# The combine stage of a soft mixture-of-experts kernel: token groups in a ring of chunks, exponentials in PSUM, row maxima spread by one fp32r product

## The reference

```python
x = x + 0.5 * ffn(layernorm(x))      # f1 in the profile
x = x + attention(layernorm(x))      # at
x = x + 0.5 * ffn(layernorm(x))      # f2

def ffn(x):
    logits   = einsum("bnd,esd->bnes", norm(x), se)
    dispatch = softmax(logits, over tokens)
    combine  = softmax(logits, over all 1024 slots)
    slots    = einsum("bnd,bnes->besd", x, dispatch)
    eout     = experts(slots)                      # [b, 1024, 256]
    return einsum("bns,bso->bno", combine, eout)   # the combine stage
```

## Time and profile before

| | |
|---|---|
| median of 3 runs | 2116.95 us (2116.89 to 2117.19) |
| profiled execution, first to last instruction | 2117.7 us; no other time is given for that execution |
| combine stage of f2, first instruction to last matmul | 1898.7 to 2112.8 us |
| PE busy | 1879.6 us, 89% |
| DVE busy | 1510.7 us, 71% |

### The profile page before, as it was taken

One profiled execution on the slowest core, in us unless ns is written; L12 is line 12 of the kernel. 1 busy time (PEld: TensorE's weight loads), 2 busy tenths in 40 slices (PEclk: granted clock), 3 DMA queues, 4 the chain that ended last, 5 costly groups with the idle time before them and its releaser, 6 DMA issues. The chain is left out here.

```text
span 2117.7 us, 35275 instructions
## 1 busy us (share of the span) xinstructions
PE 1879.6 (89%) x11782; PEld 1661.7 (78%) x11782; DVE 1510.7 (71%) x3055; ACT 1017.6 (48%) x2057; POOL 679.2 (32%) x619
## 2 busy tenths in 40 slices
PE   1799999988699899968999968999999859989999
PEld 1678787877699699968999846878778649978998
DVE  5777777763588899944555467767776348889997
ACT  0044445456455577734343302444354645547775
POOL 1422221100366455512222133212220007745553
PEclk9999999999899899988999979999999989998999
DMA  2353233320355466731212135332332115536774
GB/s 80 145 194 128 92 139 129 120 100 21 125 193 184 154 239 241 258 122 45 75 59 71 43 128 202 134 140 99 119 130 100 70 60 193 176 132 225 262 261 163
DMA packets 96785, 293.78 MB, mean 139 GB/s; under 512 B 7712, under 2 KB 47520, under 8 KB 84384
## 3 DMA queue, kind: packets, MB, share of 16 engines
q1 hardware_dynamic: 96672, 292.39, 38.9%
HBM read 183.31 MB, written 109.05 MB: 138 GB/s over the span
## 5 line engine op out<-in xcount | busy, mean ns | idle before, releaser
L76 POOL TENSOR_TENSOR pool_carrier<-minus_half 128x1 f32<-128x1 f32 x108 | 23.4, 217 | 668.9 <-DVE f2r_mv L352 289.4
L366 DVE TENSOR_SCALAR_CACHE_REDUCE f2r_lt<-f2r_ps_l,slot_shift 128x512 f32<-128x512 f32 x128 | 95.5, 747 | 87.3 <-PE f2r_ps_l L570 69.1
L366 DVE TENSOR_SCALAR_CACHE_REDUCE f1r_lt<-f1r_ps_l,slot_shift 128x512 f32<-128x512 f32 x128 | 95.5, 747 | 86.7 <-PE f1r_ps_l L570 68.6
L1122 PE MATMUL f2c_ps_y<-f2c_eo,f2c_e_hi 128*128 128x258 f32 (+1 forms) x512 | 151.0, 300 | 3.4 <-ACT f2c_e_hi L1078 3.2
L1122 PE MATMUL f1c_ps_y<-f1c_eo,f1c_e_hi 128*128 128x258 f32 (+1 forms) x512 | 151.1, 300 | 2.8 <-ACT f1c_e_hi L1078 2.7
L1123 PE MATMUL f1c_ps_y<-f1c_eo,f1c_e_hi 128*128 128x256 f32 (+1 forms) x512 | 143.8, 286 | 0.0
L1123 PE MATMUL f2c_ps_y<-f2c_eo,f2c_e_hi 128*128 128x256 f32 (+1 forms) x512 | 143.7, 286 | 0.0
L1133 PE MATMUL f1c_ps_y<-f1c_eo,f1c_e_lo 128*128 128x258 f32 (+1 forms) x512 | 135.7, 285 | 0.0
L1133 PE MATMUL f2c_ps_y<-f2c_eo,f2c_e_lo 128*128 128x258 f32 (+1 forms) x512 | 135.7, 285 | 0.0
L518 ACT ACTIVATE f2r_e_hi<-f2r_ps_t 128x512 fp32r<-128x512 f32 x128 | 69.7, 594 | 101.3 <-PE f2r_ps_t L583 101.2
L518 ACT ACTIVATE f1r_e_hi<-f1r_ps_t 128x512 fp32r<-128x512 f32 x128 | 69.7, 594 | 101.3 <-PE f1r_ps_t L583 101.2
(11 more groups left out here) (289 smaller groups left out, 6666.4 us busy)
## 6 DMA issues: line engine op xcount, KB each, us to landing
logits<-f1r_lt SPq DMA_DIRECT2D x16, 2048.0 KB, 7.3
f1c_lt<-logits SPq DMA_DIRECT2D x32, 1024.0 KB, 7.4
logits<-f2r_lt SPq DMA_DIRECT2D x16, 2048.0 KB, 7.3
f2c_lt<-logits SPq DMA_DIRECT2D x32, 1024.0 KB, 7.2
f1r_xin<-in_L_attn_x SPq DMA_DIRECT2D x16, 512.0 KB, 5.2
normalized<-f1r_xin SPq DMA_DIRECT2D x16, 512.0 KB, 2.6
f1r_xback<-normalized SPq DMA_DIRECT2D x16, 512.0 KB, 8.0
f1e_raw_g<-in_L_ffn_Wg SPq DMA_DIRECT2D x16, 512.0 KB, 4.1
```

The costliest lines, as they stand in the source:

```text
L76: pool.tensor_tensor(c["pool_carrier"][:, col:col + 1], c["minus_half"][:, 0:1], c["minus_half"][:, 0:1], ALU.add)
L366: dve.tensor_scalar(lt[:, g, sc, :], ps_l[sc % 2][:, :], c["slot_shift"][:, sc:sc + 1], None, ALU.add, ALU.max, accum_out=gmax[:, sc, g:g ...
L1122: pe.matmul(ps_y[t][:, 0:LO], e_hi[par][:, sc, tile], eo[:, bpar, sc, 0:LO], start=sc == 0, stop=False)
```

## The change

- **PE by chunks.** For chunks 0 to 5 PE takes all four tiles of a chunk in turn (`by_hi`, then `by_lo` of the chunk before). The rest (chunks 6 and 7, and `e_lo` of 5 to 7) it takes tile by tile, so that the tiles end one after the other.
- **One ring.** `e_hi` and `e_lo` have one buffer each. ACT writes chunk sc of the next group when PE has used chunk sc of this one (`chunk_used`; for 5 to 7, `mixed`).
- **One stream on the other engines.** They go from a group into the next without a break, chunk by chunk. On DVE, step sc is: F3 of the group before at sc 0; F1 at sc 7; `e_lo` of chunk sc+1 if it is DVE's; shift of chunk sc+3 (`AHEAD`); F0 after step 6, F2 after step 7. On ACT: exponential of chunk sc+1, `e_hi` of chunk sc, and after chunks 3 and 7 one `slot_out_hi`. On POOL: `e_lo` of chunks 1, 3, 5, 7, with one `slot_out_lo` after chunk 1 and one after chunk 3.
- **PSUM.** The exponentials of DVE's chunks (now 0, 2, 4, 6) are written to two PSUM banks `ps_e`, and read there for `e_hi` and `e_lo`.
- **Row maxima.** At the head of the expert stage they are split in two fp32r parts, transposed by PE and stored to memory as rows. The combine stage loads two rows for each group into a buffer of zeros, and one fp32r product with ones adds and spreads them. The diagonals on POOL go.
- **Transfers.** The logits of group i+2 are asked for in halves, each when POOL is done with that half of group i.
- **Start.** DVE does three shifts before it splits the first batch's expert outputs; PE waits for both.

```diff
+    BY_POOL = (1, 3, 5, 7)
+    TAIL = 5
+    AHEAD = 3
...
+        e_hi, e_lo = al.sb("e_hi", [P, NSC, GN], F32R), al.sb("e_lo", [P, NSC, GN], F32R)
+        ps_e = [al.ps(f"ps_e{i}", [P, BANK]) for i in range(2)]
...
 SP
+                        for h in range(2):
+                            sp.wait_ge(lo_by_pool, len(BY_POOL) * i + (h + 1) * len(BY_POOL) // 2)
+                            load_logits(i + 2, g % 2, h)
+                            if h == 0:
+                                load_max_rows(i + 2, g % 2)
...
 POOL
                     for m, sc in enumerate(BY_POOL):
+                        lo_part(i, g % 2, sc)
                         if exists(b, 0, NG) and m < NSC // NG:
                             slot_out_lo(b + 1, (b + 1) % 2, NSC // NG * g + m)
...
 DVE
+            for sc in range(AHEAD):
+                shift(0, 0, sc)
             for sc in range(NSC):
                 dve.wait_ge(eo_hi_done, sc + 1)
                 dve.tensor_tensor(eo[:, 0, sc, LO:W], eout[:, 0, sc, :], rd(eo[:, 0, sc, 0:D]), ALU.subtract)\
+            lo_part(0, 0, 0)
...
+                    for sc in range(NSC):
+                        if sc == 0 and n >= 1:
+                            finish(i - 1, (g + 1) % 2, GT - 1, n < 3)
+                        if sc == NSC - 1:
+                            finish(i, g % 2, 1, n < 2)
+                        nxt = (sc + 1) // NSC
+                        if exists(b, g, nxt) and (sc + 1) % NSC in BY_DVE:
+                            lo_part(i + nxt, (g + nxt) % 2, (sc + 1) % NSC)
+                        nxt = (sc + AHEAD) // NSC
+                        if exists(b, g, nxt):
+                            shift(i + nxt, (g + nxt) % 2, (sc + AHEAD) % NSC)
+                        if sc == NSC - 2:
+                            finish(i, g % 2, 0, n < 2)
+                        if sc == NSC - 1:
+                            finish(i, g % 2, 2, n < 2)
...
 ACT
+                if not first:
+                    if sc < TAIL:
+                        act.wait_ge(chunk_used, TAIL * (n - 1) + sc + 1)
+                    else:
+                        act.wait_ge(mixed, GT * n)
...
+                    for sc in range(NSC):
+                        nxt = (sc + 1) // NSC
+                        if exists(b, g, nxt):
+                            exponential(i + nxt, (g + nxt) % 2, (sc + 1) % NSC, known(b, g) + nxt == 0)
+                        hi_part(i, g % 2, sc, known(b, g) == 0)
+                        if exists(b, 0, NG) and sc % (NSC // 2) == NSC // 2 - 1:
+                            slot_out_hi(b + 1, (b + 1) % 2, NSC // NG * g + sc // (NSC // 2))
...
 PE
+                    for sc in range(TAIL + 1):
+                        pe.wait_ge(hi_done, NSC * i + sc + 1)
+                        for t in range(GT):
+                            if sc == 0 and known(b, g) > 0:
+                                pe.wait_ge(finished, GT * (i - 1) + t + 1)
+                            by_hi(i, bpar, t, sc)
+                        if sc >= 1:
+                            lo_ready(i, sc - 1)
+                            for t in range(GT):
+                                mm = by_lo(i, bpar, t, sc - 1)
+                            mm.then_inc(chunk_used, 1)
                     for t in range(GT):
+                        for sc in range(TAIL + 1, NSC):
+                            by_hi(i, bpar, t, sc)
+                        for sc in range(TAIL, NSC):
+                            mm = by_lo(i, bpar, t, sc)
+                        mm.then_inc(mixed, 1)
...
 expert_stage
+            act.activation(max_parts[:, 0, :], nrm, ACT.Copy).then_inc(max_hi_done, 1)
             weights_hi(0, 0, 0, True)
+            act.wait_ge(max_tr, 1)
+            act.activation(max_rows[:, :], ps_m[:, 0:P], ACT.Copy).then_inc(max_out, 1)
```

More of the change, by code:

```diff
@@ L926, in _, with load_logits, load_max_rows @@
             y_g = x_out.rearrange("b (g p t) d -> (b g) p t d", g=NG, t=GT)
[L928 to L931, removed]
+            def load_logits(n, par, h):
+                half = slice(h * NSC // 2, (h + 1) * NSC // 2)
+                sp.dma_start(lt[par][:, half, :], logits_dram[n][:, half, :]).then_inc(lt_loaded[par][h], DMA)
+            def load_max_rows(n, par):
+                sp.dma_start(rd(max_rows[par][0:2, :]), max_rows_dram[:, n, :]).then_inc(rows_loaded[par], DMA)
             def load_x(n, par):
@@ L964, in _ @@
         def _(pool):
[L965 to L971, removed]
             def lo_part(n, par, sc):
                 pool.wait_ge(hi_done, NSC * n + sc + 1)
-                pool.tensor_tensor(e_lo[par][:, sc, :], lt[par][:, sc, :], rd(e_hi[par][:, sc, :]),
+                pool.tensor_tensor(e_lo[:, sc, :], lt[par][:, sc, :], rd(e_hi[:, sc, :]),
                                    ALU.subtract).then_inc(lo_by_pool, 1)
@@ L1013, in lo_part @@
                 dve.wait_ge(hi_done, NSC * n + sc + 1)
-                dve.tensor_tensor(e_lo[par][:, sc, :], lt[par][:, sc, :], rd(e_hi[par][:, sc, :]),
+                dve.tensor_tensor(e_lo[:, sc, :], ps_e[BY_DVE.index(sc) % 2][:, :], rd(e_hi[:, sc, :]),
                                   ALU.subtract).then_inc(lo_by_dve, 1)
@@ L1053, in emit @@
                     n = known(b, g)
-                    before = (lambda: finish(i - 1, (g + 1) % 2, GT - 1, n < 3)) if n >= 1 else (lambda: None)
-                    done = lambda t: finish(i, g % 2, t, n < 2)
-                    if exists(b, g, 1):
-                        prepare(i + 1, (g + 1) % 2, before, done)
-                    else:
-                        before()
-                        for t in range(GT):
-                            done(t)
+                    for sc in range(NSC):
[13 more added lines that the diff above has]
+                            finish(i, g % 2, 2, n < 2)
             batches(dve, emit)
+            finish(LAST, 1, GT - 1, False)
         @block.scalar
@@ L1093, in emit @@
                     i = b * NG + g
-                    if exists(b, 0, NG):
-                        if g == 0 and known(b, g) > 0:
-                            act.wait_ge(mixed, NT * b)
-                        for m in range(NSC // NG):
-                            slot_out_hi(b + 1, (b + 1) % 2, NSC // NG * g + m)
-                    if exists(b, g, 1):
-                        prepare(i + 1, (g + 1) % 2, known(b, g) < 1)
+                    for sc in range(NSC):
[4 more added lines that the diff above has]
+                        if exists(b, 0, NG) and sc % (NSC // 2) == NSC // 2 - 1:
+                            if g == 0 and sc < NSC // 2 and known(b, g) > 0:
+                                act.wait_ge(mixed, NT * b)
+                            slot_out_hi(b + 1, (b + 1) % 2, NSC // NG * g + sc // (NSC // 2))
             batches(act, emit)
@@ new lines, in spread_max, with by_hi, by_lo @@
+                pe.matmul(ps_r[par][:, :], ones[:, :], max_rows[par][:, :], start=True, stop=True).then_inc(max_mm, 1)
+            def by_hi(n, bpar, t, sc):
+                tile = slice(t * P, (t + 1) * P)
+                pe.matmul(ps_y[t][:, 0:LO], e_hi[:, sc, tile], eo[:, bpar, sc, 0:LO], start=sc == 0, stop=False)
+                return pe.matmul(ps_y[t][:, 0:D], e_hi[:, sc, tile], eo[:, bpar, sc, LO:W], start=False, stop=False)
+            def by_lo(n, bpar, t, sc):
+                tile = slice(t * P, (t + 1) * P)
+                return pe.matmul(ps_y[t][:, 0:LO], e_lo[:, sc, tile], eo[:, bpar, sc, 0:LO], start=False, stop=sc == NSC - 1)
```

127 lines of the change are left out of this document (62 added, 65 removed).

## The result

The changed kernel takes 2340.94 us (median of 4 runs, 2337.84 to 2343.51), the kernel before 2116.92 beside it (4 runs): ratio 1.1062, 95% interval 1.1046 to 1.1077. The forecast was 2348, a rise of 231; the measured rise is 224.0. The profiled execution spans 2341.8 us, at a mean granted clock of 0.937 (before: 2117.7 at 0.957).

A forecast was written before the change was run, and what follows sets the result against it. PE was taken to bound the kernel, DVE 2% behind. Loops of waits and the head add 104.3 a stage, 208.6 for two, the clock 22: 2117.0 + 208.6 + 22 = 2347.6, forecast 2348 us, range 2265 to 2392.

The forecast's parts named there:

- The bound before: Combine-stage group before the change: PE bounds at 12.38 us, DVE 2% behind, with slack a group deep between them.
- The two loops: Combine-stage groups: waits between DVE and ACT, and behind POOL, make 19.9 us a group in three batches, 17.2 in the last.
- The DVE and ACT loop: Chunks 2 to 4 and 4 to 6: round trips of 3.53 us each plus 0.36 for slot_out_hi, together 7.4.
- The convoy: Chunk 6 to next chunk 0: slot_out_lo delays POOL's e_lo(5) and (7), then F0, F1: 8.0 us, last batch 5.6.
- The clock: Combine stages: PE's granted clock falls in some groups, +11 us a stage, taken as a third of all groups slow.
- the slow bound of the forecast: Combine stages with all groups at the slow clock of 1.2 GHz: +33 us for each stage.
- The head: Start of each combine stage: eight splits follow three shifts, PE starts later, partly taken back: +3 us (0 to 5).
- From chunk 0 to 2: Stretch of a combine group: e_lo(0), shifts, F2, F3, then ACT's exponential(3) and e_hi(2) before e_lo(2): 4.5 us.
- No convoy: Rival: DVE and ACT loops hold, but splitting expert outputs does not delay POOL's e_lo(5) and (7): 2266 us, chance 0.09.
- PE stays the bound: Rival: the loops hide and a combine group takes PE's 11.75 us: 2107 us, chance 0.07.

The follow-up runs named there:

- (8): Kernel before the change with only the row maxima as fp32r rows spread by one product, no POOL diagonals: 2117.78 us, ratio 1.0011.
- (9): Kernel before with the fp32r row maxima, plus exponentials of DVE's chunks (0, 2, 4, 6) in PSUM and POOL taking 1, 3, 5, 7: 2100.54 us.
- (2): Changed kernel with DVE's shifts further ahead, AHEAD = 5 in place of 3, nothing else: 2133.86 us, ratio 1.0079.
- (3): Changed kernel with AHEAD = 4 in place of 3, nothing else: 2169.42 us, ratio 1.0251.
- (6): Changed kernel with POOL's second slot_out_lo after e_lo of chunk 7 and F0 to F2 later, AHEAD left at 3: 2255.0 us, ratio 1.0663.
- (1): Changed kernel with POOL's second slot_out_lo of a group moved from after e_lo of chunk 3 to after chunk 7: 2270.01 us, ratio 1.0732.
- (10): Kernel of (5) with DVE splitting the first batch's expert outputs before its first shifts, not after: 2093.84 us, ratio 0.9893.
- (5): Changed kernel with AHEAD = 5, POOL's second slot_out_lo after e_lo of chunk 7, and F0 to F2 later: 2103.46 us, ratio 0.9938.

## Why the prediction was right

- **The bound before**: right, as far as it went. The removal of 0.63 from PE alone gained nothing (8), with DVE relieved as well it gained 16 us (9). The prediction called DVE 2% behind, 0.3 us a group; in fact DVE swallowed the whole saving.
- **The two loops**: right, and shown apart. The DVE and ACT loop: 7.47 for two pairs against 7.42 forecast, gone with a lead of 5 (2), nearly gone with 4 (3), there without the convoy (6). The convoy: forecast 2.4 a group, 53 us over 22 groups; taking it away gained 71 (1), and most of the slow clock went with it.
- **The two overlap.** The lead of 5 alone gives 207; POOL's queue and finishes alone 86 (6 against the changed kernel); all together 237.5. The remaining 55 is counted in both: a longer lead hides part of the convoy.
- **The clock**: the size was near, but not by the way that was worked out. The first 11 groups are 20.8 where 19.9 was forecast at full clock, 10 us a stage, against 11 allowed. The prediction took a third of what it would cost if slow products set the pace of a whole group, 21.2 us, and its reason for the third was that PE's work gets denser as it slows. The trace shows something else: a short stretch at 0.50 in each of these groups, behind the pause, on products that DVE waits for. No run isolated it, but its price can be read from two groups of the last batch with the same work: 17.86 at a mean clock of 0.90 and 17.00 at 1.00 in f2's stage, and in f1's 16.99 at 1.00 (979.70 to 996.69) followed by 17.87 at 0.90, so 0.9 us for one such stretch. That is about the difference between 19.9 and 20.8. So the 11 us were in part luck. This argument also misread a row: of the 66 products in the earlier trace rows 54 have 512 columns, the other 12 have 128. The Trainium skill (TensorE: Matmul & The Clock Gate, § HAM oscillation — how this bites in real kernels) describes a kernel whose clock falls at every pause between bursts. The trace bears it out for the first three batches, where each of the 11 groups has its fall, and in part for the last, with a shorter pause (DVE waits 2.4 or 2.6 before F0, not 4.5 to 5.0), where the groups of 17.00 and 16.99 stay at 1.00. None of the 11 was slow throughout, and the slow bound of the forecast, +33 a stage, was not reached.
- **The head**: near in f1's stage, over-sized in f2's. Kernel after, the head of f2's stage in order of time:

```profile
2016.22 0.76 PE L1131 MATMUL f2c_ps_r<-f2c_max_rows,f2c_ones 128*128 128x512 f32 x1 [7.43 <-DMA f2c_max_rows<-max_rows]
...
2018.82 2.77 DVE L1051 TENSOR_TENSOR f2c_eo<-f2eout,f2c_eo 128x256 fp32r<-128x256 f32 x8
...
2021.64 0.58 PE L1135 MATMUL f2c_ps_y<-f2c_eo,f2c_e_hi 128*128 128x258 f32 x1 [1.33 <-DVE f2c_eo L1051]
```

  The stage begins at 2011.48. The spread comes 4.7 us into it where 6.7 was taken, and the eight splits last 2.77 where 3.3 was; the first product stands at 10.2, not 11.9 (8.35 before). In f1's stage, which begins at 714.78, the spread comes at 5.0, the splits last 3.83 and the first product stands at 11.5 (7.7 before). To the end of group 0's products the head is longer by 2.9 in f1 and 0.6 in f2, where +3 was forecast. Its queue was rightly named (10). With all terms, a stage was forecast at 101.3 + 3 + 11 = +115.3; the two measured +115.0 and +111.5.
- **From chunk 0 to 2**: 4.25 against 4.5.
- **The rivals.** "No convoy", 2266, is nearly experiment 1's 2270, though it left out the 0.36 of `slot_out_hi` in 11 groups of each stage; with it, it would have said 2273. "PE stays the bound", 2107, is what a lead of 5 with the other queues brings (5). Each was a true description of a neighbouring kernel, told apart from this one by the order of POOL's queue, or of DVE's and POOL's.

## What to carry to other kernels

Sums of busy time by engine said that this change was worth 10 us; the round trips said that it would cost 231, and it cost 224. Where a schedule is cut to chunks, follow one resource from one use to the next through every queue, and compare that trip with the pace of the bounding engine: the lead in chunks must cover it, and here one chunk more was worth 171.5 us. Keep an instruction that waits for a late producer behind, not ahead of, those that the bounding engine needs; and before taking work from one engine, see how far behind it the next one is.

## What the runs showed of the hardware

- ACT is a little quicker with PSUM: in one stage, an exponential of 128x512 written to it takes 602 ns against 615 in SBUF, and a copy that reads PSUM 577 against 613 from SBUF (medians of 64).
- The granted clock fell to 0.50 within a group and was back at 1.00 by its last 2.5 us (a window of the kernel after from 2165.5 to 2168.0 has 1.00), at a price of 0.9 us; in the profile's view by slices of 58.5 us such stretches show only as an 8 in place of a 9.
